# Two edits in a twelve-layer Perceiver kernel: the turn of the row buffers in its expert lookup, and the order and grouping of its first loads

## What is computed

```python
# L0X, in residual form: x = x + f(layernorm(x), ctx)
q = query @ Wq.T;  gate = sigmoid(query @ Wg.T + bg)
k, v = split(kv @ Wkv.T, 2)
q, k = where(q > 0, q + 1, exp(q)), where(k > 0, k + 1, exp(k))   # per head of 16
kv_summary = einsum('bhsd,bhse->bhde', k, v);  k_sum = k.sum(-2)
out = (einsum(q, kv_summary) / (einsum(q, k_sum) + 1e-6)) * gate @ Wo.T

# L2F
h = silu(x @ W_up.T + b_up) @ W_down.T + b_down
sim = product keys against h @ W_q.T;  8 best of each half, 8 best of the 64 sums
de, ue = down_embed[indices], up_embed[indices]         # 8 heads x 8 experts
z = silu(einsum('btd,bthkd->bthk', h, de) * softmax(sc))
out = einsum('bthk,bthkd->btd', z, ue)
```

## Time and profile before

| | us |
|---|---|
| median of 3 runs | 1199.54 |
| lowest and highest | 1197.32, 1199.93 |
| the profiled execution | 1202.13 |
| its span, first to last instruction | 1199.6 |
| PE busy in it | 1059.4 (88%) |
| DVE / ACT / POOL busy | 685.6 / 486.1 / 179.2 |

### The profile page before, as it was taken

One profiled execution on the slowest core, in us unless ns is written; L12 is line 12 of the kernel. 1 busy time (PEld: TensorE's weight loads), 2 busy tenths in 40 slices (PEclk: granted clock), 3 DMA queues, 4 the chain that ended last, 5 costly groups with the idle time before them and its releaser, 6 DMA issues.

```text
span 1199.6 us, 23056 instructions
## 1 busy us (share of the span) xinstructions
PE 1059.4 (88%) x9433; PEld 747.6 (62%) x9433; DVE 685.6 (57%) x1528; ACT 486.1 (41%) x1091; POOL 179.2 (15%) x179
## 2 busy tenths in 40 slices
PE   6988899996996999999999998888999940787998
PEld 5866665665884555555555665676666630686776
DVE  3543257775336667666566652647567877556332
ACT  1111137773321344555555675533445420151332
POOL 0001300000001000000000000003776876010000
PEclk9998999997997999999999999999999975888999
DMA  9012300001202100000000000103544455005661
GB/s 382 25 52 106 122 3 2 2 2 54 119 1 92 76 1 2 2 1 2 2 2 2 2 2 30 58 13 101 143 134 144 128 138 140 16 1 203 228 224 57
DMA packets 16182, 84.38 MB, mean 70 GB/s; under 512 B 3152, under 2 KB 3664, under 8 KB 12368
## 3 DMA queue, kind: packets, MB, share of 16 engines
q1 hardware_dynamic: 7888, 57.75, 12.6%
q0 software_dynamic: 8192, 25.17, 7.5%
HBM read 82.65 MB, written 0.26 MB: 69 GB/s over the span
## 4 chain that ended last, share of the span: by engine, by line
PE 71%; DVE 14%; POOL 6%; issue 4%; ACT 2%; DMA 2%; POOLq 0%; SPq 0%; DVEq 0%; ACTq 0%
PE L2X_bank_ring L1788 7%; PE L2X_bank_ring L1804 7%; PE L2X_bank_read L1818 6%; POOL L2F_rows L2535 4%; PE L2X_bank_ring L1727 4%; PE L1X_banks_scores L916 3%; DVE x L2773 3%; PE L2X_bank_ring L1736 3%; PE L3F_bank_y L3414 2%; PE L0X_bank_k L457 2%; PE L1A_bank_qk L1181 2%; PE L0X_bank_moments L468 2%; PE L3F_bank_gate_up L3374 2%; PE L1X_bank_proj L893 2%; PE L1X_bank_read L932 2%
## 5 line engine op out<-in xcount | busy, mean ns | idle before, releaser
L2087 DVE TENSOR_REDUCE L2X_max_parts<-L2X_bank_ring 128x1 f32<-128x512 f32 x256 | 158.3, 683 | 85.7 <-PE L2X_bank_ring L1788 85.6
L1998 ACT ACTIVATE L2X_context_exp<-L2X_bank_ring 128x384 f32<-128x384 f32 (+1 forms) x384 | 144.1, 464 | 62.5 <-PE L2X_bank_ring L1804 59.6
L2535 POOL DMA_INDIRECT L2F_rows<-in_L2F_embed_dram,L2F_expert x128 | 133.0, 1039 | 63.2 <-issue 36.8
L1788 PE MATMUL L2X_bank_ring<-L2X_context_kT,L2X_q_masked 32*128 32x512 f32 x512 | 96.9, 630 | 0.0
L1024 ACT ACTIVATE L1X_probs<-L1X_clipped,L1X_drop,L1X_keep 128x1024 f32<-128x1024 f32 x64 | 77.6, 1237 | 30.7 <-DVE L1X_clipped L1084 23.5
L1084 DVE TENSOR_SCALAR L1X_clipped<-L1X_banks_scores 128x1024 f32<-128x1024 f32 x64 | 75.4, 1220 | 24.6 <-PE L1X_banks_scores L916 22.9
L1804 PE MATMUL L2X_bank_ring<-L2X_q_and_max,L2X_context_kT 32*128 32x384 f32 (+1 forms) x768 | 86.0, 498 | 0.0
L1818 PEld LDWEIGHTS L2X_bank_read<-L2X_context_exp,L2X_context_v_ones 128*32 128x32 f32 x2048 | 50.2, 109 | 43.7 <-issue 33.4
L1818 PE MATMUL L2X_bank_read<-L2X_context_exp,L2X_context_v_ones 128*32 128x128 f32 x2048 | 75.8, 277 | 1.1 <-ACT L2X_context_exp L1998 0.8
L2773 DVE SCALAR_TENSOR_TENSOR x<-L2F_rows,L2F_expert_weight,x 128x256 f32<-128x256 f32 x128 | 62.3, 487 | 4.6
L1788 PEld LDWEIGHTS L2X_bank_ring<-L2X_context_kT,L2X_q_masked 32*128 32x128 f32 x512 | 41.4, 183 | 24.1 <-issue 12.2
(11 more groups left out here) (634 smaller groups left out, 2065.3 us busy)
## 6 DMA issues: line engine op xcount, KB each, us to landing
L3F_expert_weights<-in_L3F_experts_dram SPq DMA_DIRECT2D x16, 1280.0 KB, 5.6
L1A_groups<-in_L1A_groups_dram SPq DMA_DIRECT2D x3, 1536.0 KB, 9.7
ctxT<-in_ctxT_dram SPq DMA_DIRECT2D x8, 512.0 KB, 10.6
L0X_tokens<-in_L0X_tokens_dram SPq DMA_DIRECT2D x8, 512.0 KB, 15.0
slot<-in_L1A_dram SPq DMA_DIRECT2D x1, 3584.0 KB, 11.7
slot<-in_L0F_dram SPq DMA_DIRECT2D x1, 3072.0 KB, 10.1
slot<-in_L2A_dram SPq DMA_DIRECT2D x1, 3072.0 KB, 10.6
slot<-in_L2F_dram SPq DMA_DIRECT2D x1, 2476.5 KB, 9.1
```

The costliest lines, as they stand in the source:

```text
L1788: nc.tensor.matmul(bank[:, :], qm[32 * g:32 * g + 32, b, c, j, :], cT[32 * g:32 * g + 32, s % 3, blk * 512:(blk + 1) * 512], start=True, s ...
L1998: nc.scalar.activation(ex[:, n % NE, g, 0:width(s)], bank_of(s_e, done(n) + g + 1)[:, 0:width(s)], ACT.Exp, scale=SCALE).then_inc(s_e, 1)
L2087: nc.vector.tensor_reduce(parts[:, j, g, blk:blk + 1], bank_of(s_ft, n)[:, :], AX, ALU.max).then_inc(s_ft, 1)
L2535: pool.indirect_dma_start(out=rows[:, r, k, :], out_offset=None, in_=env.dram["L2F_embed"], in_offset=bass.IndirectOffsetOnAxis(idx[:, b, ...
```

## The change

It has two parts that share nothing.

1. The ring: the three-buffer turn ends after chunk 5 instead of chunk 8. Chunk 6 goes to buffer 3 and the turn of four goes on from there (buffers 3 0 1 2 3 0 1 2 3 0 for chunks 6 to 15).
2. The first loads: the packed weights of L0X are laid out anew (Wk, Wq, Wg, Wv, Wo, bg). SP issues the key weights (256 KB), the first half of context piece 0 (256 KB), x, the constants, the other half of the piece, and the remaining weights (1152 KB), each with a semaphore of its own, and waits for none of them. The seven other context pieces move into L0X, each behind a piece of `tokens`. In L0X every engine waits for what it needs itself, and PE does `keys(1)` before q and g instead of after them.

```diff
-L0X = Fields([("Wq", KC * D), ("Wg", KC * D), ("Wkv", KC * 2 * D), ("Wo", KC * D), ("bg", D)])
+L0X = Fields([("Wk", KC * D), ("Wq", KC * D), ("Wg", KC * D), ("Wv", KC * D), ("Wo", KC * D), ("bg", D)])
...
         for j in range(B * 4):
             sp.dma_start(tokens[:, j, :, :].rearrange("p t d -> p (t d)"), env.dram["L0X_tokens"][j]).then_inc(s_tok[j], 16)
+            if j + 1 < B * 4:
+                env.load_context(sp, j + 1)
         env.issue_prefetch(sp)
...
-        env.wait_weights(pe, "L0X")
...
-            env.wait_context(pe, b, 2 * t // 4 * 4)
+            if i == 0:
+                pe.wait_ge(env.s_first, 32)
+            else:
+                env.wait_context(pe, b, 2 * t // 4 * 4)
...
         keys(0)
+        pe.wait_ge(env.s_consts, 16)
         head.tensor(pe)
+        keys(1)
+        env.wait_weights(pe, "L0X")
         pe.wait_ge(head.s_xT, 1)
         project_T(L, bank_q, wq, head.xT).then_inc(s_q, 1)
         project(L, bank_g, wg, head.xT).then_inc(s_g, 1)
-        keys(1)
...
         L.begin(pool)
+        pool.wait_ge(env.s_consts, 16)
...
+        act.wait_ge(env.s_consts, 16)
...
+        dve.wait_ge(env.s_x, 16)
         head.vector(dve, chain)
+        dve.wait_ge(env.s_consts, 16)
         k_min(0)
...
-    ring = [n % 3 for n in range(9)] + [(n + 3) % 4 for n in range(len(chunks) - 9)]
+    ring = [n % 3 for n in range(6)] + [(n + 3) % 4 for n in range(len(chunks) - 6)]
...
-                sp.dma_start(env.x[:, :, :], dram["x"].rearrange("b p d -> p b d")).then_inc(env.s_start, 16)
-                sp.dma_start(env.consts[:, :], dram["consts"]).then_inc(env.s_start, 16)
-                if env.order[0] in PACKED:
-                    env.load_weights(sp, env.order[0])
-                for j in range(B * 4):
-                    sp.dma_start(env.ctxT[:, j // 4, j % 4, :, :],
-                                 dram["ctxT"][j].rearrange("p (k t) -> p k t", k=KC)).then_inc(env.s_ctx[j], 16)
-                sp.wait_ge(env.s_start, 32)
+                half, kw, n = S2 // 8, L0X.at["Wk"][1], L0X.n
+                first, slot = dram["ctxT"][0].rearrange("p (k t) -> p k t", k=KC), env.slot("L0X")
+                sp.dma_start(slot[:, 0:kw], dram["L0X"][:, 0:kw]).then_inc(env.s_first, 16)
+                sp.dma_start(env.ctxT[:, 0, 0, :, 0:half], first[:, :, 0:half]).then_inc(env.s_first, 16)
+                sp.dma_start(env.x[:, :, :], dram["x"].rearrange("b p d -> p b d")).then_inc(env.s_x, 16)
+                sp.dma_start(env.consts[:, :], dram["consts"]).then_inc(env.s_consts, 16)
+                sp.dma_start(env.ctxT[:, 0, 0, :, half:2 * half], first[:, :, half:2 * half]).then_inc(env.s_ctx[0], 16)
+                sp.dma_start(slot[:, kw:n], dram["L0X"][:, kw:n]).then_inc(env.s_w["L0X"], 16)
```

More of the change, by code:

```diff
@@ L383, in divide @@
         return i
-L0X = Fields([("Wq", KC * D), ("Wg", KC * D), ("Wkv", KC * 2 * D), ("Wo", KC * D), ("bg", D)])
+L0X = Fields([("Wk", KC * D), ("Wq", KC * D), ("Wg", KC * D), ("Wv", KC * D), ("Wo", KC * D), ("bg", D)])
 def pack_L0X(i):
-    return [tiles(i["L0_xattn_Wq"].T), tiles(i["L0_xattn_Wg"].T), tiles(i["L0_xattn_Wkv"].T),
+    wk, wv = np.split(i["L0_xattn_Wkv"].T, 2, 1)
+    return [tiles(wk), tiles(i["L0_xattn_Wq"].T), tiles(i["L0_xattn_Wg"].T), tiles(wv),
             tiles(i["L0_xattn_Wo"].T), every_row(i["L0_xattn_bg"])]
@@ L405, in layer_L0X @@
     wg = w("Wg").rearrange("p (k n) -> p k n", k=KC)
-    wkv = w("Wkv").rearrange("p (k n) -> p k n", k=KC)
+    wk, wv = (w(n).rearrange("p (k n) -> p k n", k=KC) for n in ("Wk", "Wv"))
     VW = LinearRead.VW
@@ L478, in summary @@
                     nc.tensor.matmul(bank_s[b][:, c * VW:c * VW + P], mT[:, b, d, c * P:(c + 1) * P],
-                                     wkv[:, d, D + c * P:D + (c + 1) * P], start=(c == 0 and d == 0), stop=(d == KC - 1),
+                                     wv[:, d, c * P:(c + 1) * P], start=(c == 0 and d == 0), stop=(d == KC - 1),
                                      skip_group_check=True)
@@ L3646, in __init__ @@
         self.slots = [stack.enter_context(nc.sbuf_tensor(f"slot{j}", [P, SLOT], F32)) for j in range(2)]
-        self.s_start = stack.enter_context(nc.semaphore("x_and_consts_loaded"))
+        self.s_x, self.s_consts, self.s_first = (stack.enter_context(nc.semaphore(n)) for n in (
+            "x_loaded", "consts_loaded", "first_keys_and_context_loaded"))
         self.s_ctx = [stack.enter_context(nc.semaphore(f"context_loaded{j}")) for j in range(B * 4)]
@@ L3690, in prefetch, with load_context @@
         self.next = self.order[i] if i < len(self.order) else None
+    def load_context(self, sp, j):
+        sp.dma_start(self.ctxT[:, j // 4, j % 4, :, :],
+                     self.dram["ctxT"][j].rearrange("p (k t) -> p k t", k=KC)).then_inc(self.s_ctx[j], 16)
     def issue_prefetch(self, sp):
```

2 lines of the change are left out of this document (1 added, 1 removed).

## The result

| | before | after |
|---|---|---|
| median of 11 runs | 1201.15 | 1196.76 |
| lowest and highest | 1197.32, 1204.55 | 1188.77, 1200.55 |
| ratio, 95% interval | | 0.9948, 0.9928 to 0.9968 |
| the profiled execution, its span | 1202.13, 1199.6 | 1190.74, 1188.8 |

The change makes the kernel faster by 0.5%: 6.2 us by the ratio, with an interval of 3.8 to 8.6, where I had 12.65. The ratio isn't the quotient of the two medians, which lie 4.4 apart. The eleven times of the changed kernel form two groups, four from 1188.77 to 1191.49 and seven from 1194.71 to 1200.55, and the profiled execution is of the first. So its trace has to be read for what is in the change and what isn't.

What follows compares the result with a forecast made beforehand. PE was taken to bound the kernel, with 71% of the chain; an edit can remove its waits. Start 6.69 plus ring 5.96 gave 12.65 off the median 1199.54, so 1186.9, range 1184.0 to 1193.0.

Steps and rivals of the forecast that it cites:

- the table of landings at the start: First loads: key weights land at 3.64, half piece 4.26, x 4.88, constants 6.38, second half 7.0, remaining weights 10.02.
- the layers between keep their lengths: Layers between start and lookup: lengths unchanged, their transfers starting with their layers; so both gains reach the end.
- The ring: Lookup: chunk 8 waits for chunk 4's sum, not chunk 5's, and starts 5.96 earlier; bounds 3.9 to 6.3.
- the ring gives nothing: Lookup rival: an equal wait before chunk 8, for indices DVE makes late, replaces the old one; 1192.8, chance 0.09.
- slower: Lookup rival: chunk 9's new wait for chunk 5's sum closes a ring between POOL and DVE; 1201.9, chance 0.03.
- The start: Up to L0X's first `moments`: they start at 15.75 instead of 22.44, 6.69 less; bounds 5.1 to 6.8.
- small pieces are slow: First loads, rival: transfers with 1 KB rows run at three quarters of 414 KB per us; 1187.7, chance 0.07.
- The pause: PE between `keys(0)` and transposes: no wait, since the layer norm ends at 8.0 and `keys(0)` at 8.14.
- The slow stretch: PE's first products: eight take 3.75 instead of 1.73; if slow for 5.2 from 4.39 on, 0.7 more.
- My own sign for this: Layers between, in the changed kernel's profile: a length differing by over 2 would show the prediction wrong.
- the sum: Whole kernel: 6.69 + 5.96 = 12.65 less; the profiled execution of 1202.13 would be 1189.5, the median 1186.9.
- rivals that each take one part away whole: Start: first pieces don't land first, 1192.7, chance 0.08. Lookup: ring without gain, 1192.8, chance 0.09.

Runs made afterwards that it cites:

- experiment 2: Changed kernel with context piece 0 loaded whole, in rows of 4 KB, behind the key weights instead of its half in rows of 1 KB; ratio 0.9945 (0.9928 to 0.9963).
- experiment 3: Changed kernel with six more products on data already there, between `keys(0)` and the transposes; ratio 0.9927 (0.9902 to 0.9953).
- experiment 5: Changed kernel with idle products of constants where PE waits for VectorE in L0X's tail and L0A; 0.9911, slow chip 0.9944; with the loads of before 0.9926.

## Why the prediction was half right

The time came out at 1196.76, above the range of 1184 to 1193, and the gain is half of the 12.65. Two steps failed: the table of landings at the start, with what hangs on it, and the sentence that the layers between keep their lengths.

**The ring: right.** 5.96 predicted, 6.3 in the first pair of traces, 4.9 (3.1 to 6.7) in time. Each step can be read: chunk 8 came 23.5 behind chunk 6 (23.3 predicted), the wait of VectorE for chunk 7's exponential was 2.40 (2.0), no new wait at chunk 9, and nothing was taken back before the lookup's end. The rivals "the ring gives nothing" and "slower" are ruled out by 228.1.

**The start: the mechanism right, three terms mis-sized.** 6.69 predicted, 2.19 in the trace: the first `moments` start at 20.25, not at 15.75. In the order of the working:
- *The landings.* I priced every transfer at 393 to 414 KB per us, a rate of large transfers in a full queue. The key weights did land near 3.5, but the half piece at 6.1 instead of 4.26 (4.8 to 5.5 in the other eight traces with it), x at 6.9 instead of 4.88, the constants at 9.1 instead of 6.38. That delays the first product by 1.87 here, by 1.0 in the mean. This was my rival "small pieces are slow", and it was under-priced, at constants by 7.3. By experiment 2 it accounts for a part of the delay only. The argument that x has rows of 1 KB and still came early was weak, since the earlier trace rows shows x's landing at the head of the queue only. The Trainium skill's rule on batching ("DMA: Bandwidth & Descriptors", Bandwidth) spoke for the rival, by size. Of the two pieces of 256 KB at the head the weights, in rows of 2 KB, landed on time (2.8 after their issue); they were also the first in the queue, so this doesn't tell the row from the place.
- *The pause.* `keys(0)` covers the layer norm by 0.1 only, I wrote; with the constants late PE pauses 0.75.
- *The slow stretch.* The products stay at double time from 6.26 to 15.07, 8.8 in all, where my bound was 5.2 from the earlier trace rows. Transposes 1.09 for 0.69 and `keys(1)` 3.20 for 1.73: 1.87 more. In experiment 3 most of the pause was filled and `keys(1)` was fast; behind a pause it was slow in eleven traces of fourteen. So the pause is the likely cause, but not shown to be it. My bound took the stretch of 5.2 for the longest (by it the transposes alone would have been slow, and not half of `keys(1)`), and left out what a pause could do to it.

1.87 + 0.01 + 0.75 + 1.87 = 4.50, the whole difference between 15.75 and 20.25. A fourth thing I hadn't seen in the order of the instructions: ScalarE's wait for the constants moves its table load behind the transposes, while before it ran at 6.53, under the wait for the context. It cost nothing in this trace, since slow `keys(1)` covered it, and 0.56 of its 1.28 in the four traces where `keys(1)` was fast beside this wait. SyncE's last issue ended at 4.30 and not at 3.6; the landings came later, so this set nothing.

**"The layers between keep their lengths": wrong, in both directions.** My own sign for this, a layer that differs by over 2, is there twice: L0A by 3.9, L1X by 2.3. I took it for a matter of 1.3 to either side, from three times; it is as large as the change, and the eleven times of the kernel before spread over 7.2. It favoured the profiled execution (1190.74, 1.2 from the 1189.5 that the sum gave for it, and right for a wrong reason, so by luck), and not the median. Of the traced 8.5 the timing shows 6.2, 3.8 to 8.6, which takes in the 8.5. What is known of the loads' share beyond that one pair of traces: the first `moments` start at 23.2 in the mean of four traces with the old loads and at 19.8 of seven with the new (3.4 earlier); the way to the end of L0F is longer by 0.6 in the mean (five traces against three, much less than their spread); and L2X with L2A is 1.5 longer in the mean with ScalarE's wait. That leaves 1.3, and the timings of the loads' share are -1.2 and 0.8 (alone), 1.3 and 2.6 (changed kernel against the ring alone, on different chips), 1.8 (with idle products). All of them are near their uncertainty; that the new loads are worth 1 to 2 us is the best reading, and not shown.

**The range.** 1184 to 1193 missed 1196.76. The high end was made of rivals that each take one part away whole. The case that came, a start a third as large with its loss spread over three small terms, lay at 1199.54 - 8.5 = 1191.0 by the traces; the rest is the lengths of other layers, and the median of the kernel before itself, which moved from 1199.54 of three runs to 1201.15 of eleven.

## What to carry to other kernels

Split first loads by what the first product needs, but don't price the pieces at the rate of large transfers: the half piece, in rows of 1 KB, landed no earlier in the mean than the whole piece in rows of 4 KB. Before an engine gets a new wait, look at what stands ahead of the waiting instruction: a table load takes one of its waits and goes with it onto the path. Where an engine's clock falls in short waits, a trace against a trace says little about layers that weren't changed; feeding PE in such waits took 3.6 us away in the traces and 3 to 4 in time, half or more of what the whole change brings.

## What the runs showed of the hardware that I hadn't expected

- At PE's first products the record shows a granted clock of 1.00, and yet `keys(0)` took 3.75 or 3.78 in all but three traces (3.44, 3.48, 3.61), the length of the same products being 1.73 later. Counted with the pause behind it, the slow stretch lasted 8.8 in the changed kernel's first trace and 9.7 in that of it with idle products (experiment 5).
- In the window from 5 to 6 us the changed kernel's DMA moved 154 GB/s at a share of 0.69, the kernel with the whole first piece 388 at 0.99.
- The same instructions of L0A take 20.1, 21.5 to 22.3 or 24.0 to 24.2, in fourteen traces, with nothing in between these three groups.
- One chip of five ran the kernel before 57 us slower (1259.73 against 1202.39). In the traces of the changed kernel 66 us lie there in the layer with the 128 gathers (293.8 against 228.1), with pauses in PE's issue.
